# Folded weights ahead of the second half of the input, and that half's projections between the shifts of a convolution

## The chip, the cores and the metric

The kernel is written in Bass and runs on one core of a Trainium2 chip. The metric is the device time of one execution in microseconds (us). TensorE multiplies matrices, VectorE (DVE), ScalarE (ACT) and GpSimd (POOL) work element by element, and SyncE (SP) issues the DMAs. Each engine runs its own instruction list in order and waits on semaphores.

## The reference

The input x has 4 images of 16 x 16 pixels and 128 channels. The first of two layers, cut to what matters here:

```python
x_ln = layernorm(x, ln_g, ln_b)                        # over the 128 channels
q = x_flat @ wq + bq
q_img = q.reshape(b, c, h, w)
o = conv_general_dilated(q_img, dw_w, (2, 2), ..., feature_group_count=c)   # 7x7 depthwise, stride 2
o = gelu(o + dw_b)
offsets = conv_general_dilated(o, pw_w, (1, 1), ...)   # 128 -> 2 channels
deformed = refs + tanh(offsets)
interp = grid_sample_bilinear_zeros(x, grid of deformed)
v = k = interp_flat @ wv + bv
qh = heads(q @ mq_w + mq_b); kh = heads(k @ mk_w + mk_b); vh = heads(v @ mv_w + mv_b)
att = softmax(qh kh^T) vh
z = att @ mo_w + mo_b + x
x = gelu(layernorm(z) @ mlp_w + mlp_b) + z
```

The second layer is a group norm, one attention head of width 128 over the 256 pixels of an image, an output projection and a residual.

## The kernel before, in words

All data fits on chip. x lies in eight tiles of 128 pixels by 128 channels (two tiles an image), and the work up to the sampling goes in two halves of two images, four tiles each. Everything is float32 apart from dummy matmuls on zeros (`keep_warm`, on the bfloat16 tile `warm`). A float32 matmul shows as two passes in the trace, each with a weight load, so 4 matmuls are 8 rows there. The order of every engine is written out by hand.

**Loads.** SP issues (lines 246 to 255) image 0, image 1, the constants `early`, a row of biases, then the second half of x in one DMA of 256 KB (semaphore `x_in2`), then the 320 KB of weights `fold` (`fold_in`), then `gb`, `mid`, `x_st` and `late`.

**Norm and first projection.** DVE takes statistics of the four tiles of a half (`st`, `mv`), ACT takes the square root (`sd`), DVE the reciprocal (`rstd`). The normalized tiles `x_hat` of the first half come from DVE (line 540), those of the second half from ACT (line 363), which needs `shift` from DVE (line 545). TensorE projects each tile with `wq_conv`: one 128 x 128 matmul, in which the tile is the stationary operand (loop at line 872). `qbias_mm` is a bias made by TensorE and copied by ACT to `q_bias`. DVE's `project_images(g)` (line 511) writes `q_conv` for the two images of half g.

**Convolution as matmuls.** `move_half(g)` (line 825) spreads `q_conv` over partitions with 16 matmuls that have 32 output partitions each; ACT and DVE copy the result to `q_ph` (`phases_out`, two phases each). `conv_half(g, first, last)` (line 843) runs shifts first to last-1 of 16 shifts, four matmuls of 32 output partitions a shift, all into bank 5. Their weights `wd` are made by POOL in four chunks (line 280). Moves and shifts show as form `128*32`, full matmuls as `128*128`. After the sixteenth shift of half 0, ACT applies the GELU (`o_act`, line 372), TensorE makes the coordinates (`coord_half`), ACT the tanh, and DVE, ACT the bilinear weights with which TensorE samples x.

**Folded weights.** `fold_keys` (line 860) multiplies `wv` into `mk_w` and `mv_w` (one matmul of 256 columns); `fold_query` (line 865) multiplies `wq` into `mq_w` and makes three bias columns with one-column matmuls. ACT copies `m_kv`, `m_q` and `cols` out of the banks (lines 389 to 398).

**TensorE's order before.** Project tiles 0 to 3 (bias before tile 3), two dummy matmuls, `move_half(0)`, `fold_query`, project tiles 4 to 7, shifts 0 to 5 of half 0, `move_half(1)`, shifts 6 to 15, `fold_keys`, `coord_half(0)`, then the first five shifts of half 1, the queries of half 0, and the sampling. Later stages (scores, softmax, MLP, group norm, second attention) are not touched.

Of the kernel before, what the change touches and what calls it, by code (L numbers as in the profile page):

```python
# [8 lines left out]
ACT = mybir.ActivationFunctionType  # L9
# [3 lines left out]
B, H, W, C = 4, 16, 16, 128  # L13
# [55 lines left out]
def build(nc, x, early, fold, mid, late, rows, ln_rows, out):  # L69
    ctx = ExitStack()  # L70
    with ctx:
# [27 lines left out]
        def r(name):  # L99
# [78 lines left out]
            "loads and constants": """x_in0 x_in1 x_in2 early_in fold_in mid_in late_in rows_in lnrow_in xst_in  # L178
                warm_set ones_set consts vones_set v1ones_set""",
            "norm of x": "stats aggr sdev rstd_ok shift_ok hat_ok hat_a xg_ok xln_ok",  # L180
            "folded weights": """colsum_mm colsum_ok qbias_mm qbias_ok foldq_mm m_q_ok cols_ok foldkv_mm m_kv_ok
                fold1_mm w_vo_ok cols1_ok outbias_mm outbias_ok msabias_mm msabias_ok mlpw_ok gamma_ok""",
            "convolution": """q_mm q_out wd_ok move_a move_v qph_a qph_v conv_mm gelu_ok""",
            "sampling": "coord_mm tanh_ok dx_ok dy_ok fx_ok ay_ok hx_ok hy_ok bilin_ok interp_mm sampled_ok",
# [15 lines left out]
        def halves(h):  # L200
            return slice(4 * h, 4 * h + 4)
# [41 lines left out]
        @block.sync  # L243
        def _(sp):

            for b in range(G):
                sp.dma_start(x_hw[:, S * b:S * b + S, :], x_hw_dram[:, b]).then_inc(s[f"x_in{b}"], 16)  # L247
            sp.dma_start(packs["early"][:, :], early).then_inc(s["early_in"], 16)
            sp.dma_start(row[:, :], rows).then_inc(s["rows_in"], 16)
            sp.dma_start(x_hw[:, halves(1), :].rearrange("p (b s) c -> p b s c", s=S), x_hw_dram[:, G:B]).then_inc(s["x_in2"], 16)  # L250
            sp.dma_start(packs["fold"][:, :], fold).then_inc(s["fold_in"], 16)
            sp.dma_start(gb[:, :], ln_rows.partition_broadcast(P)).then_inc(s["lnrow_in"], 16)
            sp.dma_start(packs["mid"][:, :], mid).then_inc(s["mid_in"], 16)
            sp.dma_start(x_st[:, :, :], x_st_dram).then_inc(s["xst_in"], 16)
            sp.dma_start(packs["late"][:, :], late).then_inc(s["late_in"], 16)

            for b in range(B - 1):
                sp.wait_ge(s["y_ok"], 2 * b + 2)
                sp.dma_start(out_dram[:, b, :], y[:, 2 * b:2 * b + 2, :].rearrange("p s c -> p (s c)")).then_inc(s["y_out"], 16)
            for i in (T - 2, T - 1):  # L260
                sp.wait_ge(s["y_ok"], i + 1)
                t = i % S
                sp.dma_start(out_dram[:, B - 1, t * C:(t + 1) * C], y[:, i, :]).then_inc(s["y_out"], 16)

            sp.wait_ge(s["y_out"], 16 * (B + 1))

        @block.gpsimd
        def _(pool):
# [15 lines left out]
            def norm_affine(h):  # L284
# [63 lines left out]
        def _(act):  # L348
# [6 lines left out]
            act.wait_ge(s["qbias_mm"], 1)  # L355
            act.copy(q_bias[:, :].rearrange("c (r s n) -> c r s n", r=2, s=S),
                     bank[5][:, 0:C].rearrange("c (r n) -> c r n", r=2).unsqueeze(2).to_broadcast([P, 2, S, C // 2])).then_inc(s["qbias_ok"], 1)
            act.wait_ge(s["aggr"], 8)
            act.activation(sd[:, halves(1)], mv[:, halves(1), 1], ACT.Sqrt, bias=eps[:, 0:1]).then_inc(s["sdev"], 1)
            act.wait_ge(s["shift_ok"], 1)  # L360

            for i in range(4, T):
                act.activation(x_hat[:, i], x_hw[:, i], ACT.Identity, scale=rstd[:, i:i + 1],
                               bias=shift[:, i - 4:i - 3]).then_inc(s["hat_a"], 1)

            def phases_out(g):
                act.wait_ge(s["move_a"], g + 1)
# [15 lines left out]
                act.activation(hat_y[:, g].rearrange("p s q -> p (s q)"), abs_y[:, g], ACT.Relu, scale=-1.0, bias=1.0).then_inc(s["hy_ok"], 1)  # L383

            phases_out(0)
            act.activation(scratch[:, 1:2], eps[:, :], ACT.Gelu)
            phases_out(1)
            gelu_half(0)
            act.wait_ge(s["foldkv_mm"], 1)
            act.copy(m_kv[:, :], bank[7][:, 0:2 * C]).then_inc(s["m_kv_ok"], 1)  # L390
            tanh_half(0)

            act.wait_ge(s["foldq_mm"], 1)
            act.copy(m_q[:, :], bank[6][:, 0:C]).then_inc(s["m_q_ok"], 1)
# [115 lines left out]
        def _(dve):  # L510
# [9 lines left out]
                        op0=ALU.mult, op1=ALU.add).then_inc(s["q_out"], 1)  # L520


            for h in range(2):
                for i in range(4 * h, 4 * h + 4):
                    if i in (0, 2, 4):

                        dve.wait_ge(s[f"x_in{i // 2}"], 16)
                    dve.bn_stats(st[:, i], x_hw[:, i]).then_inc(s["stats"], 1)  # L528
                for i in range(4 * h, 4 * h + 4):
                    dve.wait_ge(s["stats"], i + 1)  # L530
                    dve.bn_aggr(mv[:, i], st[:, i]).then_inc(s["aggr"], 1)
                if h == 1:
                    dve.wait_ge(s["early_in"], 16)
                    project_images(0)
                dve.wait_ge(s["sdev"], h + 1)
                dve.reciprocal(rstd[:, halves(h)], sd[:, halves(h)]).then_inc(s["rstd_ok"], 1)
                dve.wait_ge(s["rstd_ok"], h + 1)
                if h == 0:
                    for i in range(4):
                        dve.tensor_scalar(x_hat[:, i], x_hw[:, i], mv[:, i, 0:1], rstd[:, i:i + 1], ALU.subtract, ALU.mult).then_inc(s["hat_ok"], 1)  # L540
                    dve.wait_ge(s["colsum_mm"], 1)
                    dve.tensor_copy(colsum[:, :], bank[5][0:1, 0:C]).then_inc(s["colsum_ok"], 1)
                else:

                    dve.scalar_tensor_tensor(out=shift[:, :], in0=mv[:, halves(1), 0], scalar=-1.0, in1=rstd[:, halves(1)],
                                             op0=ALU.mult, op1=ALU.mult).then_inc(s["shift_ok"], 1)

            def phases_out(g):
                dve.wait_ge(s["move_v"], g + 1)
                dve.tensor_copy(q_ph[:, g, 2:4].rearrange("p k n -> p (k n)"), bank[4][:, 0:2 * G * PIX]).then_inc(s["qph_v"], 1)  # L550

            phases_out(0)
            project_images(1)
            phases_out(1)

# [252 lines left out]
        def _(pe):  # L808
# [13 lines left out]
            mm(bank[5][0:1, 0:C], ones_col[:, :], w("wq_conv")).then_inc(s["colsum_mm"], 1)  # L822
            keep_warm(2)

            def move_half(g):

                pe.wait_ge(s["q_out"], G * g + G)
                if g == 1:

                    pe.wait_ge(s["qph_a"], 1)  # L830
                    pe.wait_ge(s["qph_v"], 1)
                src = q_conv[:, g].rearrange("c (r yb t x) -> c r yb t x", r=2, t=2, x=OW)
                for k in range(PHASES):
                    at = (k % 2) * G * PIX
                    for f in range(PHASES):
                        m = mm(bank[3 + k // 2][f * BLK:(f + 1) * BLK, at:at + G * PIX].rearrange("p (yb x) -> p yb x", x=OW),
                               w("ident")[:, k * BLK:(k + 1) * BLK], src[:, f // 2, :, f % 2])
                    if k == 1:
                        m.then_inc(s["move_a"], 1)
                    if k == 3:  # L840
                        m.then_inc(s["move_v"], 1)
# [22 lines left out]

            def fold_query():
                pe.wait_ge(s["fold_in"], 16)
                mm(bank[6][:, 0:C], w("wqT"), w("mq_w"))
                mm(bank[6][:, C:C + 1], w("mq_w"), w("bq"))
                mm(bank[6][:, C + 1:C + 2], w("mk_w"), w("bv"))
                mm(bank[6][:, C + 2:C + 3], w("mv_w"), w("bv")).then_inc(s["foldq_mm"], 1)  # L870

            for i in range(T):
                b, t = divmod(i, S)
                if i == 3:

                    pe.wait_ge(s["colsum_ok"], 1)
                    pe.wait_ge(s["rows_in"], 16)
                    mm(bank[5][:, 0:C], r("ln_b"), colsum[:, :], stop=False)
                    mm(bank[5][:, 0:C], ones_row[:, :], r("bq_conv"), start=False).then_inc(s["qbias_mm"], 1)
                if i == 4:  # L880
                    keep_warm(2)
                    move_half(0)
                    fold_query()

                if i < 4:
                    pe.wait_ge(s["hat_ok"], i + 1)
                else:
                    pe.wait_ge(s["hat_a"], i - 3)
                o = query_image(b).rearrange("c (r s n) -> c r s n", r=2, s=S)[:, :, t]
                m = mm(o, x_hat[:, i], w("wq_conv"))  # L890
                if t == S - 1:
                    m.then_inc(s["q_mm"], 1)

            def query_half(h):
                pe.wait_ge(s["m_q_ok"], 1)
# [133 lines left out]
                mm(bank[3 + b][:, 0:HW], mlp_wg[:, :], z_t[:, 2 * b:2 * b + 2, :].rearrange("c s q -> c (s q)")).then_inc(s["mlp_mm"], 1)  # L1029

            N = len(SHIFTS)
            conv_half(0, 0, 6)
            move_half(1)
            conv_half(0, 6, N)
            fold_keys()
            coord_half(0)
            conv_half(1, 0, 5)
            query_half(0)
# [254 lines left out]
```

## Time and profile before

| | us |
|---|---|
| runs | 79.25, 79.36, 79.98; median 79.36 |
| the profiled execution | 79.27 |
| its span, first to last instruction | 77.4 |
| around the span | 1.87 |
| PE, DVE, ACT, POOL busy | 70.6, 51.7, 33.9, 24.3 |

The span is what the instructions of the program cover. Of the 77.4 us, this case concerns the stretch from about 2.5 to 19 us. A pass of TensorE has a modelled end: its next pass starts before that end when the two overlap in the array.

### The profile page before, as it was taken

Reading aid. Unit: us, or ns where it says so; the run is one execution under the profiler, and the core shown is the slowest. Engines: PE = TensorE matmul, PEld = TensorE weight load, DVE = VectorE, ACT = ScalarE, POOL = GpSimd, SP = SyncE. Lnnn points to the kernel's source line nnn. Section 1 sums busy time; section 2 is a strip of 40 time slices with the busy share of each in tenths; the row PEclk is TensorE's granted clock in tenths of the full one; section 3 lists DMA queues with packets and bytes.
Section 4 is the critical chain, followed back from the end, with each engine's and each line's share of the span. In section 5 each row is a group of like instructions: output and inputs, shape, how many; then the busy total and the mean of one; then the engine's idle time right before and its main releaser. Section 6 shows DMA issues by size and latency. Waiting matters only on the chain.

```text
span 77.4 us, 1968 instructions
## 1 busy us (share of the span) xinstructions
PE 70.6 (91%) x732; PEld 53.6 (69%) x732; DVE 51.7 (67%) x172; ACT 33.9 (44%) x84; POOL 24.3 (31%) x37
## 2 busy tenths in 40 slices
PE   4999699998999999999999999998897999998950
PEld 2345599783786647879777989845485869996830
DVE  0478742116366959477789968599799786868480
ACT  6112397068139563524424419820248048263600
POOL 5008999900000038390019137123820030000000
PEclk9999999999999999999999999999999999999999
DMA  0789870000000000000000000000000000010112
GB/s 9 226 270 150 305 289 12 0 8 0 0 8 0 0 0 4 0 0 8 0 0 0 4 0 0 8 0 0 0 0 0 0 0 4 0 68 9 59 55 89
DMA packets 3051, 3.07 MB, mean 40 GB/s; under 512 B 225, under 2 KB 2657, under 8 KB 3042
## 3 DMA queue, kind: packets, MB, share of 16 engines
q1 hardware_dynamic: 3042, 2.95, 12.8%
q8 instruction: 6, 0.10, 0.5%
q14 instruction: 3, 0.02, 0.1%
HBM read 2.42 MB, written 0.52 MB: 38 GB/s over the span
## 4 chain that ended last, share of the span: by engine, by line
PE 63%; DVE 17%; issue 5%; DMA 5%; ACT 3%; SPq 2%; POOL 2%; DVEq 0%; POOLq 0%; ACTq 0%
PE bank L810 53%; DMA x_hw<-x 5%; PE bank L971 5%; PE bank L1140 2%; DVE smax L604 2%; DVE x_t L656 1%; DVE gst L694 1%; SPq L247 1%; DVE st L528 1%; DVE bilin L578 1%; DVE x_gn L716 1%; DVE dist_y L562 1%; PE bank L989 1%; DVE q_conv L517 1%; POOL grs L330 1%
## 5 line engine op out<-in xcount | busy, mean ns | idle before, releaser
L810 PE MATMUL bank<-k_blk,qh 128*128 128x512 f32 x16 | 8.4, 605 | 0.0
L810 PE MATMUL bank<-v_blk,p_t 128*128 128x34 f32 x64 | 7.8, 267 | 0.0
L810 PEld LDWEIGHTS bank<-v_blk,p_t 128*128 128x128 f32 x64 | 7.8, 192 | 0.0
L810 PE MATMUL bank<-warm 128*128 128x512 bf16 x18 | 6.3, 471 | 1.0 <-POOL warm L269 1.0
L604 DVE TENSOR_REDUCE smax<-bank 128x8 f32<-128x512 f32 x8 | 5.5, 685 | 2.4 <-PE bank L810 2.4
L317 POOL TENSOR_TENSOR zrs<-zve,neg_half 128x2 f32<-128x2 f32 x4 | 2.9, 714 | 12.7 <-DVE zve L646 12.7
L810 PE MATMUL bank<-q_ph,wd 128*32 128x112 f32 (+5 forms) x256 | 6.8, 249 | 0.0
L303 POOL TENSOR_TENSOR x_res<-x_st,msa_bias 128x1024 f32<-128x1024 f32 x1 | 2.4, 2358 | 12.8 <-DVE bilin L578 12.8
L431 ACT ACTIVATE p_t<-bank 128x512 f32<-128x512 f32 x8 | 4.8, 597 | 3.4 <-PE bank L971 3.4
L810 PEld LDWEIGHTS bank<-q_ph,wd 128*32 128x32 f32 x256 | 5.6, 109 | 0.7 <-issue 0.3
L611 DVE TENSOR_TENSOR s_sub<-bank,smax 128x512 f32<-128x512 f32 x8 | 5.5, 682 | 0.1
L280 POOL TENSOR_TENSOR wd<-pack_early 128x512 f32<-128x512 f32 x4 | 4.1, 1046 | 4.4 <-DVE x_hat L540 4.4
L810 PE MATMUL bank<-v,p_t 128*128 128x129 f32 x32 | 4.8, 284 | 0.6 <-ACT p_t L233 0.4
L810 PEld LDWEIGHTS bank<-v,p_t 128*128 128x128 f32 x32 | 4.2, 190 | 1.2 <-issue 1.0
L971 PE MATMUL bank<-pack_early,s_sub 128*128 128x128 f32 x32 | 5.0, 279 | 0.0
L488 ACT ACTIVATE p<-bank,nmax 128x256 f32<-128x256 f32 x8 | 3.4, 476 | 3.0 <-DVE nmax L728 2.8
L438 ACT COPY att_t<-bank 128x128 f32<-128x128 f32 x8 | 2.1, 263 | 5.4 <-PE bank L989 5.3
L971 PEld LDWEIGHTS bank<-pack_early,s_sub 128*128 128x128 f32 x32 | 3.7, 144 | 0.8 <-issue 0.5
L810 PE MATMUL bank<-k,q 128*128 128x256 f32 x16 | 4.2, 385 | 0.0
L528 DVE BATCH_NORM_STATS2 st<-x_hw 128x6 f32<-128x128 f32 x8 | 1.8, 283 | 3.2 <-DMA x_hw<-x 3.2
L810 PEld LDWEIGHTS bank<-warm 128*128 128x128 bf16 x18 | 2.0, 122 | 2.9 <-issue 1.9
L810 PE MATMUL bank<-pack_mid,att_t 128*128 128x128 f32 x16 | 3.7, 311 | 0.2 <-DVE z L634 0.2
(149 smaller groups left out, 161.2 us busy)
## 6 DMA issues: line engine op xcount, KB each, us to landing
x_st<-x SPq DMA_DIRECT2D x1, 512.0 KB, 6.7
pack_late<-late SPq DMA_DIRECT2D x1, 448.0 KB, 7.3
out<-y SPq DMA_DIRECT2D x3, 128.0 KB, 1.7
pack_fold<-fold SPq DMA_DIRECT2D x1, 320.0 KB, 4.1
pack_mid<-mid SPq DMA_DIRECT2D x1, 261.0 KB, 5.8
x_hw<-x SPq DMA_DIRECT2D x2, 128.0 KB, 2.2
x_hw<-x SPq DMA_DIRECT2D x1, 256.0 KB, 3.8
pack_early<-early SPq DMA_DIRECT2D x1, 184.0 KB, 2.5
```

The costliest lines, as they stand in the source:

```text
L280: pool.tensor_tensor(wd[:, n:n + WD_CHUNK].rearrange("p n k j -> p (n k) j"), w("ident32").unsqueeze(1).to_broadcast([P, WD_CHUNK * PHASES ...
L303: pool.tensor_tensor(x_res[:, :, :], x_st[:, :, :].rearrange("p b (s c) -> p (b s) c", s=S), msa_bias[:, :].unsqueeze(1).to_broadcast([P, ...
L317: pool.tensor_tensor(zrs[:, 2 * b:2 * b + 2], zve[:, 2 * b:2 * b + 2], neg_half[:, 0:2], ALU.pow).then_inc(s["zrs_ok"], 1)
L431: act.activation(p_t[:, i % 2].rearrange("p j q -> p (j q)"), bank[5 + i % 2][:, :], ACT.Exp).then_inc(s["exp_ok"], 1)
L438: act.copy(att_t[:, i % 2], bank[0][:, 0:P]).then_inc(s["attt_ok"], 1)
L488: act.activation(p1[:, b % 2, t], bank[5 + b % 2][:, t * HW:(t + 1) * HW], ACT.Exp, bias=nmax1[:, 2 * b + t:2 * b + t + 1]).then_inc(s["p1 ...
L528: dve.bn_stats(st[:, i], x_hw[:, i]).then_inc(s["stats"], 1)
L604: dve.tensor_reduce(smax[:, i % 2], scores(i), AX.X, ALU.max).then_inc(s["smax_ok"], 1)
L611: dve.tensor_tensor(s_sub[:, i % 2], scores(i), smax[:, i % 2].unsqueeze(2).to_broadcast([P, NH, PIX]), ALU.subtract).then_inc(s["ssub_ok" ...
L810: return pe.matmul(o, l, r_, start=start, stop=stop, **k)
L971: m = pe.transpose(bank[5 + i % 2][:, j * P:(j + 1) * P], s_sub[:, i % 2, 2 * j:2 * j + 2].rearrange("p h q -> p (h q)"), w("ident"))
L1140: m = pe.transpose(bank[(2, 0)[t]][:, j * P:(j + 1) * P], p1[:, b % 2, t, j * P:(j + 1) * P], w("ident"))
```

## The change

SP issues `fold` ahead of the second half of x. On TensorE the two dummy matmuls ahead of the first move go; both folds stand in their place, and the three bias columns follow the first move as `fold_columns`, with a wait for `m_q_ok` since they share a bank with the product that ACT copies. The projections of tiles 4 to 7 go between shifts of half 0 (after 5, 7, 9 and 11 shifts), and `move_half(1)` is cut in two: phases 0 and 1 after 14 shifts, phases 2 and 3 after the sixteenth. On DVE `project_images(0)` goes ahead of the second half's statistics, and the scale and shift of the second half go behind `phases_out(0)`. ACT copies `m_kv` and `m_q` ahead of `phases_out(0)` and makes the four `x_hat` tiles behind it. POOL waits for `shift_ok` before its `norm_affine(0)`. The amount of arithmetic is the same apart from the two dummy matmuls.

```diff
             sp.dma_start(row[:, :], rows).then_inc(s["rows_in"], 16)
+            sp.dma_start(packs["fold"][:, :], fold).then_inc(s["fold_in"], 16)
             sp.dma_start(x_hw[:, halves(1), :].rearrange("p (b s) c -> p b s c", s=S), x_hw_dram[:, G:B]).then_inc(s["x_in2"], 16)
-            sp.dma_start(packs["fold"][:, :], fold).then_inc(s["fold_in"], 16)
...
+            pool.wait_ge(s["shift_ok"], 1)
             norm_affine(0)
...
-            act.wait_ge(s["aggr"], 8)
...
+            act.wait_ge(s["foldkv_mm"], 1)
+            act.copy(m_kv[:, :], bank[7][:, 0:2 * C]).then_inc(s["m_kv_ok"], 1)
+            act.wait_ge(s["foldq_mm"], 1)
+            act.copy(m_q[:, :], bank[6][:, 0:C]).then_inc(s["m_q_ok"], 1)
...
             phases_out(0)
+            act.wait_ge(s["aggr"], 8)
...
+            dve.wait_ge(s["early_in"], 16)
+            project_images(0)
+            input_stats(1)
             phases_out(0)
+            input_scale(1)
...
+            for i in range(3):
+                project_tile(i)
...
+            project_tile(3)
+            fold_keys()
+            fold_query()
+            move_half(0)
+            fold_columns()
...
-            conv_half(0, 0, 6)
-            move_half(1)
-            conv_half(0, 6, N)
-            fold_keys()
+            conv_half(0, 0, 5)
+            project_tile(4)
+            conv_half(0, 5, 7)
+            project_tile(5)
+            conv_half(0, 7, 9)
+            project_tile(6)
+            conv_half(0, 9, 11)
+            project_tile(7)
+            conv_half(0, 11, 14)
+            move_half(1, range(0, 2))
+            conv_half(0, 14, N)
+            move_half(1, range(2, 4))
             coord_half(0)
```

TensorE before, from the last tile of the first half to the coordinates (`pack_fold` are the folds, `q_conv` the moves, `q_ph,wd` the shifts, `o_act` the coordinates):

```order
8 L810 MATMUL bank<-pack_early,x_hat 128x2x64 [waits hat_ok]
9 L810 MATMUL bank<-warm 128x512 x2
10 L810 MATMUL bank<-q_conv,pack_early 32x128 [waits q_out]
11 L810 MATMUL bank<-q_conv,pack_early 32x128 x15
12 L810 MATMUL bank<-pack_fold 128x128 [waits fold_in]
13 L810 MATMUL bank<-pack_early,pack_fold 128x1 x3
14 L810 MATMUL bank<-pack_early,x_hat 128x2x64 [waits hat_a] x4
15 L810 MATMUL bank<-q_ph,wd 32x128 [waits wd_ok,qph_v,qph_a]
...
36 L810 MATMUL bank<-pack_fold 128x256 [waits fold_in]
37 L810 MATMUL bank<-o_act,pack_early 128x128 [waits gelu_ok]
```

And the same engine in the changed kernel, up to the third of the four projections that now stand among the shifts:

```order
8 L814 MATMUL bank<-pack_early,x_hat 128x2x64 [waits hat_ok]
9 L814 MATMUL bank<-pack_fold 128x256 [waits fold_in]
10 L814 MATMUL bank<-pack_fold 128x128 [waits fold_in]
11 L814 MATMUL bank<-q_conv,pack_early 32x128 [waits q_out]
12 L814 MATMUL bank<-q_conv,pack_early 32x128 x15
13 L814 MATMUL bank<-pack_early,pack_fold 128x1 [waits m_q_ok]
...
22 L814 MATMUL bank<-pack_early,x_hat 128x2x64 [waits hat_a]
23 L814 MATMUL bank<-q_ph,wd 32x14x6 x4
24 L814 MATMUL bank<-q_ph,wd 32x14x7 x4
25 L814 MATMUL bank<-pack_early,x_hat 128x2x64 [waits hat_a]
26 L814 MATMUL bank<-q_ph,wd 32x112 x4
27 L814 MATMUL bank<-q_ph,wd 32x14x7 [waits wd_ok]
```

The two folds took the place of the dummy matmuls, and each projection of the second half now stands alone between matmuls with 32 output partitions.

DVE before, in the same stretch (`st` and `mv` are the second half's statistics, `q_ph` the copy that the first shift needs):

```order
10 L528 BN_STATS st<-x_hw 128x6 [waits x_in2]
11 L528 BN_STATS st<-x_hw 128x6 x3
12 L531 BN_AGGR mv<-st 128x2 [waits stats] x4
13 L517 SCALAR_TENSOR_TENSOR q_conv<-bank,pack_early,q_bias 128x16x16 [waits q_mm,qbias_ok,early_in]
14 L517 SCALAR_TENSOR_TENSOR q_conv<-bank,pack_early,q_bias 128x16x16 [waits q_mm]
15 L536 RECIPROCAL rstd<-sd 128x4 [waits sdev]
16 L545 SCALAR_TENSOR_TENSOR shift<-mv,rstd 128x4 [waits rstd_ok]
17 L550 COPY q_ph<-bank 128x256 [waits move_v]
```

DVE in the changed kernel:

```order
10 L518 SCALAR_TENSOR_TENSOR q_conv<-bank,pack_early,q_bias 128x16x16 [waits q_mm,qbias_ok,early_in]
11 L518 SCALAR_TENSOR_TENSOR q_conv<-bank,pack_early,q_bias 128x16x16 [waits q_mm]
12 L529 BN_STATS st<-x_hw 128x6 [waits x_in2]
13 L529 BN_STATS st<-x_hw 128x6 x3
14 L532 BN_AGGR mv<-st 128x2 [waits stats] x4
15 L541 COPY q_ph<-bank 128x256 [waits move_v]
16 L536 RECIPROCAL rstd<-sd 128x4 [waits sdev]
17 L555 SCALAR_TENSOR_TENSOR shift<-mv,rstd 128x4 [waits rstd_ok]
```

The statistics moved behind the first half's `q_conv`, and the reciprocal and `shift` behind the copy to `q_ph`.

## Rows read from the trace of the kernel before

**Rows 1.** The page: busy time, and the granted clock in forty slices.

```profile
PE 70.6 (91%) x732; PEld 53.6 (69%) x732; DVE 51.7 (67%) x172; ACT 33.9 (44%) x84; POOL 24.3 (31%) x37
PEclk9999999999999999999999999999999999999999
```

**Rows 2.** Chain that ended last, in time: start us, us, what.

```profile
2.58 3.76 DMA x_hw<-x
...
8.38 6.58 PE bank L810 x195
```

**Rows 3.** Timeline of TensorE: start us, us, what, count [idle before].

```profile
6.80 0.49 PE L810 MATMUL bank<-pack_early,x_hat 128*128 128x128 f32 x2
7.13 0.59 PE L810 MATMUL bank<-warm 128*128 128x512 bf16 x2
8.38 1.08 PE L810 MATMUL bank<-q_conv,pack_early 128*32 128x128 f32 x32 [0.65 <-DVE q_conv L517]
9.39 0.49 PE L810 MATMUL bank<-pack_fold 128*128 128x128 f32 x2
9.71 0.73 PE L810 MATMUL bank<-pack_early,pack_fold 128*128 128x1 f32 x6
10.30 1.14 PE L810 MATMUL bank<-pack_early,x_hat 128*128 128x128 f32 x8
11.37 1.15 PE L810 MATMUL bank<-q_ph,wd 128*32 128x128 f32 x48
12.34 1.06 PE L810 MATMUL bank<-q_conv,pack_early 128*32 128x128 f32 x32
13.21 2.35 PE L810 MATMUL bank<-q_ph,wd 128*32 128x98 f32 x80
15.49 0.70 PE L810 MATMUL bank<-pack_fold 128*128 128x256 f32 x2
16.02 0.71 PE L810 MATMUL bank<-o_act,pack_early 128*128 128x128 f32 x4
19.72 0.71 PE L810 MATMUL bank<-q_ph,wd 128*32 128x84 f32 x24
20.36 0.49 PE L810 MATMUL bank<-sampled,m_kv 128*128 128x128 f32 x2
20.78 0.45 PE L810 MATMUL bank<-m_kv,sampled 128*64 128x64 f32 x8
```

**Rows 4.** Timeline of ScalarE, same columns.

```profile
6.91 0.37 ACT L356 COPY q_bias<-bank 128x256 f32<-128x256 f32 x1 [2.35 <-PE bank L810]
9.18 1.65 ACT L363 ACTIVATE x_hat<-x_hw,shift,rstd 128x128 f32<-128x128 f32 x4 [1.33 <-DVE shift L545]
15.61 0.37 ACT L372 ACTIVATE o_act<-bank,pack_early 128x128 f32<-128x128 f32 x1 [2.21 <-PE bank L810]
```

**Rows 5.** Timeline of VectorE, same columns.

```profile
6.36 0.87 DVE L528 BATCH_NORM_STATS2 st<-x_hw 128x6 f32<-128x128 f32 x4 [0.25 <-DMA x_hw<-x]
7.16 0.36 DVE L531 BATCH_NORM_AGGREGATE mv<-st 128x2 f32<-128x6 f32 x4
7.45 0.88 DVE L517 SCALAR_TENSOR_TENSOR q_conv<-bank,pack_early,q_bias 128x256 f32<-128x256 f32 x2
8.44 0.71 DVE L545 SCALAR_TENSOR_TENSOR shift<-mv,rstd 128x4 f32<-128x4 f32 x1
9.53 0.42 DVE L550 COPY q_ph<-bank 128x256 f32<-128x256 f32 x1 [0.38 <-PE bank L810]
```

**Rows 6.** Timeline of GpSimd: the convolution weights, four chunks.

```profile
6.08 4.06 POOL L280 TENSOR_TENSOR wd<-pack_early 128x512 f32<-128x512 f32 x4 [4.42 <-DVE x_hat L540]
```

**Rows 7.** DMA issues, KB and us from issue to landing; before them SyncE's issue of fold.

```profile
3.01 0.50 SPq L251 DMA_DIRECT2D pack_fold<-fold  x1
...
pack_fold<-fold SPq DMA_DIRECT2D x1, 320.0 KB, 4.1
gb<-ln_rows SPq DMA_DIRECT2D x1, 128.0 KB, 5.0
```

More of the change, by code:

```diff
@@ L180, in build @@
             "norm of x": "stats aggr sdev rstd_ok shift_ok hat_ok hat_a xg_ok xln_ok",
-            "folded weights": """colsum_mm colsum_ok qbias_mm qbias_ok foldq_mm m_q_ok cols_ok foldkv_mm m_kv_ok
+            "folded weights": """colsum_mm colsum_ok qbias_mm qbias_ok foldq_mm foldc_mm m_q_ok cols_ok foldkv_mm m_kv_ok
                 fold1_mm w_vo_ok cols1_ok outbias_mm outbias_ok msabias_mm msabias_ok mlpw_ok gamma_ok""",
@@ L357, in _ @@
                      bank[5][:, 0:C].rearrange("c (r n) -> c r n", r=2).unsqueeze(2).to_broadcast([P, 2, S, C // 2])).then_inc(s["qbias_ok"], 1)
-            act.wait_ge(s["aggr"], 8)
[L359 to L364, printed above, removed]
+            act.wait_ge(s["foldkv_mm"], 1)
+            act.copy(m_kv[:, :], bank[7][:, 0:2 * C]).then_inc(s["m_kv_ok"], 1)
+            act.wait_ge(s["foldq_mm"], 1)
+            act.copy(m_q[:, :], bank[6][:, 0:C]).then_inc(s["m_q_ok"], 1)
             def phases_out(g):
@@ L385, in _ @@
             phases_out(0)
+            act.wait_ge(s["aggr"], 8)
+            act.activation(sd[:, halves(1)], mv[:, halves(1), 1], ACT.Sqrt, bias=eps[:, 0:1]).then_inc(s["sdev"], 1)
+            act.wait_ge(s["shift_ok"], 1)
+            for i in range(4, T):
+                act.activation(x_hat[:, i], x_hw[:, i], ACT.Identity, scale=rstd[:, i:i + 1],
+                               bias=shift[:, i - 4:i - 3]).then_inc(s["hat_a"], 1)
             act.activation(scratch[:, 1:2], eps[:, :], ACT.Gelu)
@@ L388, in _ @@
             gelu_half(0)
-            act.wait_ge(s["foldkv_mm"], 1)
-            act.copy(m_kv[:, :], bank[7][:, 0:2 * C]).then_inc(s["m_kv_ok"], 1)
             tanh_half(0)
-            act.wait_ge(s["foldq_mm"], 1)
-            act.copy(m_q[:, :], bank[6][:, 0:C]).then_inc(s["m_q_ok"], 1)
             hats_half(0)
+            act.wait_ge(s["foldc_mm"], 1)
             for j, name in enumerate(("mq_b", "mk_b", "mv_b")):
@@ L520, in project_images, with input_stats @@
                         op0=ALU.mult, op1=ALU.add).then_inc(s["q_out"], 1)
-            for h in range(2):
+            def input_stats(h):
                 for i in range(4 * h, 4 * h + 4):
@@ L531, in _, with input_scale @@
                     dve.bn_aggr(mv[:, i], st[:, i]).then_inc(s["aggr"], 1)
-                if h == 1:
-                    dve.wait_ge(s["early_in"], 16)
-                    project_images(0)
+            def input_scale(h):
                 dve.wait_ge(s["sdev"], h + 1)
@@ L537, in _ @@
                 dve.wait_ge(s["rstd_ok"], h + 1)
[L538 to L546, printed above, removed]
             def phases_out(g):
@@ L550, in phases_out @@
                 dve.tensor_copy(q_ph[:, g, 2:4].rearrange("p k n -> p (k n)"), bank[4][:, 0:2 * G * PIX]).then_inc(s["qph_v"], 1)
+            input_stats(0)
+            input_scale(0)
+            for i in range(4):
+                dve.tensor_scalar(x_hat[:, i], x_hw[:, i], mv[:, i, 0:1], rstd[:, i:i + 1], ALU.subtract, ALU.mult).then_inc(s["hat_ok"], 1)
+            dve.wait_ge(s["colsum_mm"], 1)
+            dve.tensor_copy(colsum[:, :], bank[5][0:1, 0:C]).then_inc(s["colsum_ok"], 1)
+            dve.wait_ge(s["early_in"], 16)
+            project_images(0)
+            input_stats(1)
             phases_out(0)
+            input_scale(1)
+            dve.scalar_tensor_tensor(out=shift[:, :], in0=mv[:, halves(1), 0], scalar=-1.0, in1=rstd[:, halves(1)],
+                                     op0=ALU.mult, op1=ALU.mult).then_inc(s["shift_ok"], 1)
             project_images(1)
@@ L823, in _, with move_half @@
             keep_warm(2)
-            def move_half(g):
+            def move_half(g, phases=range(PHASES)):
                 pe.wait_ge(s["q_out"], G * g + G)
@@ L832, in move_half @@
                 src = q_conv[:, g].rearrange("c (r yb t x) -> c r yb t x", r=2, t=2, x=OW)
-                for k in range(PHASES):
+                for k in phases:
                     at = (k % 2) * G * PIX
@@ L866, in fold_query, with fold_columns, project_tile @@
                 pe.wait_ge(s["fold_in"], 16)
-                mm(bank[6][:, 0:C], w("wqT"), w("mq_w"))
+                mm(bank[6][:, 0:C], w("wqT"), w("mq_w")).then_inc(s["foldq_mm"], 1)
+            def fold_columns():
+                pe.wait_ge(s["m_q_ok"], 1)
                 mm(bank[6][:, C:C + 1], w("mq_w"), w("bq"))
                 mm(bank[6][:, C + 1:C + 2], w("mk_w"), w("bv"))
-                mm(bank[6][:, C + 2:C + 3], w("mv_w"), w("bv")).then_inc(s["foldq_mm"], 1)
-            for i in range(T):
+                mm(bank[6][:, C + 2:C + 3], w("mv_w"), w("bv")).then_inc(s["foldc_mm"], 1)
+            def project_tile(i):
                 b, t = divmod(i, S)
[L874 to L883, printed above, removed]
                 if i < 4:
@@ L892, in _ @@
                     m.then_inc(s["q_mm"], 1)
+            for i in range(3):
+                project_tile(i)
+            pe.wait_ge(s["colsum_ok"], 1)
+            pe.wait_ge(s["rows_in"], 16)
+            mm(bank[5][:, 0:C], r("ln_b"), colsum[:, :], stop=False)
+            mm(bank[5][:, 0:C], ones_row[:, :], r("bq_conv"), start=False).then_inc(s["qbias_mm"], 1)
+            project_tile(3)
[3 more added lines that the diff above has]
+            fold_columns()
             def query_half(h):
```

## The prediction

> **What bounds the kernel now.** I read the busy time by engine first: TensorE is busy for 70.6 of 77.4 us, with VectorE next at 51.7, and the granted clock is at its upper level (2.4 GHz) in all forty slices [rows 1]. Then the chain that ended last: it comes from the landing of x's second half at 6.34 us (2.58 + 3.76), through VectorE's statistics and `q_conv`, to TensorE at 8.38, and stays on TensorE for 195 passes [rows 2]. Then TensorE's timeline, which tells which of its work stands in front of the convolution's end [rows 3]. From 8.38 to 16.02 it idles nowhere for a wait: move 8.38, fold 9.39, columns 9.71, four projected tiles 10.30, six shifts 11.37, the second move 12.34, ten shifts 13.21 (ending 13.21 + 2.35 = 15.56). What follows hangs on that end: the GELU runs 15.61 to 15.98 [rows 4] and the coordinates start at 16.02. `fold_keys`, at 15.49, stands in the GELU's shadow and costs nothing where it is. So the question is when the sixteenth shift of half 0 ends. All later stages wait for things derived from it, with nothing else late there, so they move by the same amount; I found nothing of theirs that the change touches.
>
> **The head of the stretch.** `q_bias` is ready at 6.91 + 0.37 = 7.28 [rows 4], but `q_conv` starts only at 7.45, since VectorE is on the statistics [rows 5]. Changed, it starts at 7.32 and ends at 7.32 + 0.88 = 8.20; TensorE's first move follows at 8.25 instead of 8.38. The gain is 0.13. The folds must fit ahead of it. They start at 7.13, where the dummy matmuls do, if `fold` has landed: issued at 2.58 instead of 3.01, with 4.1 to landing [rows 7], it lands by 6.7 (2.58 + 3.76 = 6.3 by the other transfer of about that size [rows 2]). Added without overlap, 0.70 and 0.49 [rows 3] end at 8.32, but a pass of the same form starts about 0.16 before the modelled end of the last, so 8.0 is nearer; the next form may start then. They cost nothing. If they were late by 0.1 the move is late by 0.1. Without the dummies TensorE idles 0.25 here; the idle 0.65 of before [rows 3] did not lower the granted clock [rows 1], so I charge nothing.
>
> **From the first move to the first shift.** Move: 8.25 + 1.08 = 9.33. The columns start 0.07 before that (the move's row ends at 9.46, the next starts at 9.39 [rows 3]), at 9.26; `m_q`, which they wait for, is copied about 8.25 to 8.55. They keep TensorE 0.73, plus 0.09 because the first pass after a change of form waits for its weights (see below): 10.08 to 10.17. The shifts start 0.07 before that, 10.10. Is VectorE in time? Statistics run 6.36 to 7.52 in before, 1.16 [rows 5]; behind `q_conv` they end at 8.20 + 1.18 = 9.38. The last move pass ends about 9.33 and the copy to `q_ph` takes 0.42 [rows 5], so it is done at 9.82. It binds nothing, with 0.28 to spare. POOL's first chunk of weights is long there [rows 6]. First shift: 10.10 instead of 11.37, a gain of 1.27, of which the four tiles that went elsewhere are 1.07 (10.30 to 11.37).
>
> **What a projected tile costs among the shifts.** This decides the case. Within one form the next row starts well before the modelled end of the one before: shifts end 11.37 + 1.15 = 12.52, the move starts 12.34, 0.18 earlier. Where the form changes, the overlap is 0.07 each time: shifts end 20.43 and the full matmul starts 20.36; it ends 20.85 and the next form starts 20.78; the tiles end 11.44 and the shifts start 11.37 [rows 3]. A lone 128 x 128 matmul is 0.49 (20.36), while in a row of four it is 1.07 / 4 = 0.27. So let shifts end at E. The tile starts at E - 0.07, ends at E + 0.42, and the next shift starts at E + 0.35. Without the tile it would have started at E - 0.18. That is 0.53, and I take 0.55 because the first weights of the new form are not loaded ahead. Four tiles: 2.20, against 1.07 where they stood. Its bounds: 0.27 (the in-row slot) and 0.67 (no overlap at all: 0.49 + 0.18).
>
> What the rows show is thus a price of some 0.11 for each change between 32, 64 and 128 output partitions, and the change adds eight of them. The Trainium skill, "TensorEngine Tiling (Array Packing)", Key Properties, says the same in principle: changing the tiling mode, not just the tile, drains TensorE. By that rule no clever order of independent work hides it and 0.55 stands; without the rule, a tile at 0.27 is open and the sum below would be 1.1 lower. The trace agrees with the rule at every change of form that I looked at.
>
> **The second move.** Before, all of it (12.34 to 13.21, 0.87) stands ahead of the last shift. Now half does; the other half runs in the GELU's shadow. The GELU path from the last shift's end to the coordinates is 16.02 - 15.56 = 0.46, and half a move is 0.44. Gain 0.43, and the coordinates stay bound by the GELU. VectorE's copy of that half (0.42) ends about 0.9 after the last shift, and the first shift of half 1 comes 1.1 after it (16.02 + 0.71 - 0.07 = 16.66, less 15.56), so it is covered too, by 0.2.
>
> **The waits that are added.** Tile 4 needs ACT's first `x_hat`. VectorE makes `shift` after the copy: reciprocal 9.84 to 10.01, shift from 10.04. Before, `shift` took 0.71 for 4 columns, from 8.44 to 9.15, while POOL worked at `wd` [rows 5, 6]; POOL's third chunk (four in 4.06) ends at about 9.13. The fourth ends at 10.14, and now POOL then waits, so I let `shift` end by 10.25, and the first `x_hat` by 10.75 (four take 1.65 [rows 4], about 0.48 for one). TensorE gets to tile 4 at 10.10 + 5 x 0.16 = 10.90 (six shifts took 11.37 to 12.34). No wait, 0.15 to spare. The other tiles come every 0.4 for ACT and every 0.9 for TensorE. Behind ACT's tiles stands one table load, as before, and its next copy is not due before about 15. POOL's part of the queries comes 0.1 to 0.2 later and is needed only after five shifts of half 1.
> `shift` reads two SBUF tiles. The Trainium skill, "SBUF — State Buffer", Who interferes with whom, has VectorE's instructions with two SBUF inputs held off by a GpSimd instruction until it is over. The row agrees with that (0.71, ending with a chunk); by it `shift` is done just after 10.14, otherwise it would be 0.71 by itself and end at 10.75, which is rival 3.
> The move at 14 shifts needs `q_conv` of image 3: after tile 7 VectorE takes about 0.48 for one image plus 0.07 of signalling; TensorE has three shifts, about 0.5, less the 0.07 overlap. I charge 0.10.
>
> **The sum.** End of shift sixteen: 10.10 + 4.19 (11.37 to 15.56) - 0.43 + 2.20 + 0.10 = 16.16, against 15.56: 0.60 later. The parts: head and tiles moved away -1.27, half move -0.43, four lone tiles +2.20, wait +0.10. The profiled execution took 79.27 (span 77.4, 1.87 around it), so 79.87, said as 79.9. The runs' median, 79.36, is 0.09 above the profiled one; against it the forecast is +0.7%, inside the 1% (0.79 us) that a measurement of this kernel can tell from no change.
>
> **Rivals.**
> 1. *The change of form is hidden*: shifts and tile are independent and a tile costs its in-row 0.27. Then 4 x 0.27 = 1.08 in place of 2.20: 16.16 - 1.12 = 15.04, 0.52 earlier, 78.75; by start-to-start times a tile in a row is less (a pair of passes is 0.49 and eight are 1.14, so six more are 0.65, or 0.22 a tile), which takes 0.20 more, to 78.55. For it: rows only show modelled ends. Against: starts are measured, and 20.36 to 20.78 is this very pattern.
> 2. *x's second half lands late* and VectorE's in-order queue then holds back the copy to `q_ph`, which before did not stand behind that data. Issued at about 3.1, with 3.76 it lands at 6.9; with the 5.0 of the transfer behind it [rows 7] at 8.1. It decides from 10.10 - 0.04 - 0.42 - 0.04 - 1.16 = 8.44 on, one for one. At 9.8 the end would be 1.36 later: 81.2. Against: 320 KB ahead of it instead of behind is a bandwidth matter of 1 us at most, as fold landed 0.8 after it before.
> 3. *`shift` is slow by itself*, 0.71 wherever it stands: first `x_hat` at 10.75 + 0.03 + 0.48 = 11.26, TensorE waits 0.35 at tile 4, the sum is 80.2. This is slower than before by 1.1%. It decides from a first `x_hat` after 10.90. For it: I have the one row.
> 4. *The fold lands too late* for 7.13: every tenth past 7.4 delays the first move by one. At before's 7.1 it costs nothing, so 79.9 stays.
>
> **How the numbers follow.** The forecast has 0.62, within 79.5 to 80.4: the tile price may be 0.50 or 0.60 (0.2 each way) and small waits add up to 0.2. About a fifth of it lies above 80.15. Rival 1 has 0.15, most of it faster by over 1%. Rival 3 has 0.13, two thirds of it slower by over 1%. Rival 2 has 0.05, all slower. Rival 4 and what I don't see have 0.05, nearly all within 1%. Faster: 0.12 + 0.01 = 0.13. Slower: 0.13 + 0.09 + 0.05 = 0.27. Same: 0.60. The range, 79.0 to 80.6, takes in the tile at about 0.35 below and rival 3 with small waits above; it leaves out rival 1 in full and rival 2.
>
> **What would show it.** In the changed profile: moves start at 8.25; the first shift at 10.1 (11.37 before); each `x_hat` pair of passes between shifts spans 0.49 with 0.07 of overlap on both sides; the last shift of half 0 ends near 16.2 and the coordinates start near 16.6; the sampling is 0.6 later, and so is every later stage. The forecast is wrong if a lone tile takes less than 0.4 from shift to shift, if the first shift starts after 10.3, or if some later stage doesn't move with the sampling.

## The result and the profile after

The changed kernel takes 79.95 us in the median (79.51 to 80.36, 20 runs), the kernel before 79.42 (78.95 to 80.00, 20 runs): ratio 1.0061, 95% interval 1.0037 to 1.0085. It is slower by 0.6%, a half microsecond. The profiled execution took 80.20, its span is 78.4. The medians and ratios of this document leave out executions that took over 1.5% more than the fastest of the same kernel.

TensorE after, in the stretch of [rows 3] (columns as there):

```profile
7.62 0.49 PE L814 MATMUL bank<-pack_early,x_hat 128*128 128x128 f32 x2
7.95 0.82 PE L814 MATMUL bank<-pack_fold 128*128 128x256 f32 x4
9.18 1.08 PE L814 MATMUL bank<-q_conv,pack_early 128*32 128x128 f32 x32 [0.42 <-DVE q_conv L518]
10.19 0.83 PE L814 MATMUL bank<-pack_early,pack_fold 128*128 128x1 f32 x6
10.95 1.01 PE L814 MATMUL bank<-q_ph,wd 128*32 128x128 f32 x40
11.89 0.49 PE L814 MATMUL bank<-pack_early,x_hat 128*128 128x128 f32 x2
12.31 0.52 PE L814 MATMUL bank<-q_ph,wd 128*32 128x84 f32 x16
...
14.59 0.49 PE L814 MATMUL bank<-pack_early,x_hat 128*128 128x128 f32 x2
15.01 0.71 PE L814 MATMUL bank<-q_ph,wd 128*32 128x112 f32 x24
15.65 0.65 PE L814 MATMUL bank<-q_conv,pack_early 128*32 128x128 f32 x16
16.11 0.55 PE L814 MATMUL bank<-q_ph,wd 128*32 128x112 f32 x16
16.47 0.62 PE L814 MATMUL bank<-q_conv,pack_early 128*32 128x128 f32 x16
17.14 0.71 PE L814 MATMUL bank<-o_act,pack_early 128*128 128x128 f32 x4
...
20.21 0.70 PE L814 MATMUL bank<-x_hw,bilin 128*64 128x64 f32 x16 [0.37 <-DVE bilin L582]
```

VectorE after, answering to [rows 5]:

```profile
8.25 0.88 DVE L518 SCALAR_TENSOR_TENSOR q_conv<-bank,pack_early,q_bias 128x256 f32<-128x256 f32 x2 [2.21 <-PE bank L814]
9.05 0.86 DVE L529 BATCH_NORM_STATS2 st<-x_hw 128x6 f32<-128x128 f32 x4
...
10.33 0.42 DVE L541 COPY q_ph<-bank 128x256 f32<-128x256 f32 x1
10.67 0.17 DVE L536 RECIPROCAL rstd<-sd 128x4 f32<-128x4 f32 x1
10.88 0.16 DVE L555 SCALAR_TENSOR_TENSOR shift<-mv,rstd 128x4 f32<-128x4 f32 x1
...
15.11 0.48 DVE L518 SCALAR_TENSOR_TENSOR q_conv<-bank,pack_early,q_bias 128x256 f32<-128x256 f32 x1 [1.26 <-PE bank L814]
```

ScalarE after, answering to [rows 4], and the landing of the fold:

```profile
11.07 1.65 ACT L389 ACTIVATE x_hat<-x_hw,shift,rstd 128x128 f32<-128x128 f32 x4 [0.55 <-DVE shift L555]
...
16.36 0.37 ACT L366 COPY q_ph<-bank 128x256 f32<-128x256 f32 x1 [2.13 <-PE bank L814]
16.73 0.37 ACT L370 ACTIVATE o_act<-bank,pack_early 128x128 f32<-128x128 f32 x1
```

```profile
pack_fold<-fold SPq DMA_DIRECT2D x1, 320.0 KB, 3.7
```

Absolute times mislead here. The first move starts at 9.18 against 8.38 [rows 3], yet the tile three places ahead of it starts at 7.62 against 6.80: 0.8 us were already lost in front of the first instruction that differs on TensorE. The two dummy matmuls before the first tiles show where. This is the kernel before, and after:

```profile
4.68 0.60 PE L810 MATMUL bank<-warm 128*128 128x512 bf16 x2
```

```profile
5.02 1.03 PE L814 MATMUL bank<-warm 128*128 128x512 bf16 x2
```

The same two instructions take 0.60 in one profile and 1.03 in the other. It is not work that the change added, since TensorE's instructions up to there are the same in both kernels (more on it at the end). So I read every profile from the start of the first move, and call the time from there to the coordinates "the stretch". It is 16.02 - 8.38 = 7.64 in the first profile of before and 17.14 - 9.18 = 7.96 after. From the coordinates to the sampling both have 3.07, and from the sampling to the end of the span 58.3 and 58.2: nothing later answers to the change.

In the stretch, the first shift starts 1.77 after the first move (2.99 before). From the first shift to the end of the sixteenth it takes 16.66 - 10.95 = 5.71 (4.19 before). A tile among the shifts reads 11.89 to 12.38, with 0.07 of overlap with its neighbour on each side.

### The profile page after: what moved, and what is told of

It is laid out like the page before. It is cut to its first block, busy times and chain, and to the rows that moved or that the text cites. A ratio compares the mean times of both kernels' runs of the same rounds, so it can differ in the third digit from the quotient of the medians.

```text
span 78.4 us, 1965 instructions
## 1 busy us (share of the span) xinstructions
PE 72.1 (92%) x730; PEld 54.1 (69%) x730; DVE 51.3 (65%) x172; ACT 33.9 (43%) x84; POOL 24.3 (31%) x37
## 2 busy tenths in 40 slices
DMA packets 3051, 3.07 MB, mean 39 GB/s; under 512 B 225, under 2 KB 2657, under 8 KB 3042
## 4 chain that ended last, share of the span: by engine, by line
PE 70%; DVE 15%; issue 5%; ACT 4%; POOL 2%; DVEq 0%; POOLq 0%; ACTq 0%
PE bank L814 61%; PE bank L979 5%; PE bank L1156 2%; DVE smax L608 2%; DVE x_t L660 1%; DVE gst L698 1%; DVE q_conv L518 1%; DVE bilin L582 1%; DVE x_gn L720 1%; DVE dist_y L566 1%; PE bank L997 1%; POOL grs L331 1%; DVE s_sub L615 1%; POOL zrs L318 1%; DVE x_res L665 1%
## 5 line engine op out<-in xcount | busy, mean ns | idle before, releaser
L814 PE MATMUL bank<-q_ph,wd 128*32 128x84 f32 (+5 forms) x256 | 7.2, 251 | 0.0
L518 DVE SCALAR_TENSOR_TENSOR q_conv<-bank,pack_early,q_bias 128x256 f32<-128x256 f32 x4 | 1.8, 481 | 5.8 <-PE bank L814 5.8
```

The source lines that it names most:

```text
L518: dve.scalar_tensor_tensor(out=q_conv[:, g].rearrange("c (n b x) -> c n b x", b=G, x=R * OW)[:, :, b % G], in0=query_image(b).rearrange("c ...
L814: return pe.matmul(o, l, r_, start=start, stop=stop, **k)
```

## The experiments

Ratios are to the kernel before, timed on the same chip. The stretch is from each one's profile. e9, a single timed run of e5's kernel, stands with e5 below.

| kernel | median us | ratio, interval | stretch us |
|---|---|---|---|
| changed | 79.95 | 1.0061 (1.0037 to 1.0085) | 7.96 |
| e1 one block | 78.83 | 0.9930 (0.9898 to 0.9963) | 6.82 |
| e11 two pairs | 79.26 | 0.9969 (0.9937 to 1.0001) | 7.30 |
| e2 move whole | 80.28 | 1.0123 (1.0085 to 1.0160) | 8.39 |
| e3 four extra, spread | 81.56 | 1.0282 (1.0233 to 1.0331) | 9.48 |
| e4 four extra, together | 80.20 | 1.0102 (1.0061 to 1.0143) | 8.48 |
| e10 before again | one run, 78.94 | | 7.25 |
| e6 before, fold first | 79.53 | 1.0022 (0.9994 to 1.0050) | 7.25 |
| e7 changed, x first | 80.20 | 1.0107 (1.0064 to 1.0151) | 7.96 |
| e5 no POOL wait | 80.45 | 1.0162 (1.0114 to 1.0210) | 7.96 |
| e8 block, keys late | 78.85 | 0.9931 (0.9902 to 0.9961) | 6.73 |

**e1: the four tiles in one block.**

```diff
-            conv_half(0, 0, 5)
-            project_tile(4)
...
-            conv_half(0, 9, 11)
-            project_tile(7)
-            conv_half(0, 11, 14)
+            conv_half(0, 0, 9)
+            for i in range(4, T):
+                project_tile(i)
+            conv_half(0, 9, 14)
```

> The changed kernel with the four projections of the second half in one block after nine shifts, in place of four places. My theory (each change of form costs about 0.11 us, so three tiles fall from 0.55 to 0.22 us): 1.0 us less than the changed kernel, 78.9 to 79.0, ratio to before about 0.994. A small loss of 0.1 is possible if the moves wait for q_conv of image 3. If instead the loss came from something else (the DMA order, the split move, the removed dummy matmuls), it stays at 79.9 to 80.0, ratio 1.006.

Measured 78.83, 1.1 us less than the changed kernel. The shifts, the block and the shifts behind it, of this kernel:

```profile
10.58 1.68 PE L814 MATMUL bank<-q_ph,wd 128*32 128x128 f32 x72
12.19 1.16 PE L814 MATMUL bank<-pack_early,x_hat 128*128 128x128 f32 x8
13.28 1.07 PE L814 MATMUL bank<-q_ph,wd 128*32 128x96 f32 x40
```

Four tiles take 1.09 from start to the next start; spread out each takes 0.42 plus a lost overlap. This kernel beats both, and before by 0.7%.

**e11: two pairs** (tiles 4 and 5 after 7 shifts, 6 and 7 after 11).

```diff
-            conv_half(0, 0, 5)
-            project_tile(4)
...
+            conv_half(0, 0, 7)
+            project_tile(4)
+            project_tile(5)
+            conv_half(0, 7, 11)
+            project_tile(6)
+            project_tile(7)
```

> The changed kernel with the four projections in two pairs, after 7 and after 11 shifts: two pairs of form changes fewer than the changed kernel, one pair more than the block. Theory (0.33 us for each pair of changes): first move to coordinates 7.96 - 0.66 = 7.30 in the profile (the wait for image 3 may add 0.15 or less), 79.3 in the median, ratio 0.999. Rival (only the number of places beyond one matters, or the wait for q_conv carried the gain of the block): 78.9 or 79.9.

The stretch is 16.27 - 8.97 = 7.30, as expected, and the median 79.26. Four places, two places, one place: 7.96, 7.30, 6.82. The first two places given up are worth 0.33 each, the third 0.48. Of that the wait for image 3 is 0.15: it is in the two spread kernels and not in the block, where the move starts 0.19 before the shifts ahead of it end.

```profile
11.99 0.71 PE L814 MATMUL bank<-pack_early,x_hat 128*128 128x128 f32 x4
12.63 0.92 PE L814 MATMUL bank<-q_ph,wd 128*32 128x112 f32 x32
...
16.27 0.71 PE L814 MATMUL bank<-o_act,pack_early 128*128 128x128 f32 x4
```

**e3 and e4: the price by itself.** Four matmuls whose result nobody reads, in the kernel before.

```diff
+            def extra():
+                mm(bank[7][:, 2 * C:3 * C], w("ident"), w("wq_conv"))
...
-            conv_half(0, 6, N)
+            conv_half(0, 6, 7)
+            extra()
+            conv_half(0, 7, 9)
+            extra()
...
```

> The kernel before with four extra full matmuls of 128 x 128 (result unused, bank 7), each alone between shifts of half 0 (after 7, 9, 11 and 13). Measures the disputed price by itself. My theory: 4 x 0.55 = 2.2 us more, 81.6, ratio 1.028. Rival (a change of form is hidden): 4 x 0.22 = 0.9 us, 80.3, ratio 1.011.

> The kernel before with the same four extra matmuls in one block after nine shifts. My theory: 0.55 + 3 x 0.22 = 1.2 us more, 80.6, ratio 1.015, so 1.0 us less than spread. Rival (a change of form is hidden): the same 80.3 as spread.

Against the stretch of 7.25 of the kernel before (e10), spread costs 9.48 - 7.25 = 2.23 and together 8.48 - 7.25 = 1.23. The medians, against 79.28 for the kernel before on that chip, say 2.3 and 0.9. The 0.9 is under the 1.2 that was expected and that the profile shows, and its interval (0.5 to 1.1) leaves 1.2 out; why the timed runs lost less stays open. The rival is out all the same: equal work in another order differs by 1.0 in the stretches and by 1.4 in the medians. One extra of the spread kernel, then the block of the other:

```profile
13.77 0.49 PE L810 MATMUL bank<-pack_early 128*128 128x128 f32 x2
14.19 0.57 PE L810 MATMUL bank<-q_ph,wd 128*32 128x112 f32 x16
```

```profile
14.33 1.16 PE L810 MATMUL bank<-pack_early 128*128 128x128 f32 x8
15.42 1.43 PE L810 MATMUL bank<-q_ph,wd 128*32 128x96 f32 x56
```

**e2: the second move whole.**

```diff
-            move_half(1, range(0, 2))
-            conv_half(0, 14, N)
-            move_half(1, range(2, 4))
+            move_half(1)
+            conv_half(0, 14, N)
```

> The changed kernel with the second move whole, after 14 shifts, so that no half of it runs in the GELU's shadow. My theory: the second half of the move stands ahead of the last shift again, 0.43 us more than the changed kernel, 80.4, ratio 1.012. Rival (the coordinates are held by ScalarE's copy of q_ph ahead of the GELU, or the whole is bound elsewhere): no more than 0.1 us of difference.

Measured 80.28. That is 1.00 above the kernel before on its chip, where the changed kernel is 0.53 above, so 0.47 more, and 8.39 - 7.96 = 0.43 in the stretch. The half in the GELU's shadow is really hidden: without it TensorE idles 0.49 there.

```profile
16.15 0.54 PE L814 MATMUL bank<-q_ph,wd 128*32 128x112 f32 x16
17.18 0.71 PE L814 MATMUL bank<-o_act,pack_early 128*128 128x128 f32 x4 [0.49 <-ACT o_act L370]
```

**e10: before again.** No edit.

> The kernel before, unchanged, for a second profile. In the first one shifts 6 to 15 of half 0 took 2.28 us from start to the fold behind them, with a gap of 0.28 that nothing released; the same stretch took 1.86 with the fold's DMA moved. If the gap is a chance of that one run, first move to coordinates takes 7.25 here instead of 7.64, and the changed kernel's 7.96 is 0.71 longer. If it belongs to the kernel, 7.64 again.

The gap did not come again. The first row starts 1.86 before the fold behind it, where [rows 3] has 2.28:

```profile
13.26 1.93 PE L810 MATMUL bank<-q_ph,wd 128*32 128x98 f32 x80
15.12 0.70 PE L810 MATMUL bank<-pack_fold 128*128 128x256 f32 x2
```

In the first profile of before, the gap shows among the weight loads (PEld) of the same shifts:

```profile
13.10 1.62 PEld L810 LDWEIGHTS bank<-q_ph,wd 128*32 128x32 f32 x68
15.00 0.34 PEld L810 LDWEIGHTS bank<-q_ph,wd 128*32 128x32 f32 x12 [0.28 <-issue]
```

So the changed kernel's stretch is 7.96 - 7.25 = 0.71 longer, not 0.32.

**e6 and e7: the order of the DMAs alone**, in before and in the changed kernel (the second swaps them back).

```diff
+            sp.dma_start(packs["fold"][:, :], fold).then_inc(s["fold_in"], 16)
             sp.dma_start(x_hw[:, halves(1), :].rearrange("p (b s) c -> p b s c", s=S), x_hw_dram[:, G:B]).then_inc(s["x_in2"], 16)
-            sp.dma_start(packs["fold"][:, :], fold).then_inc(s["fold_in"], 16)
```

> The kernel before with the fold's DMA ahead of the second half of x, and nothing else. VectorE still takes the statistics first. Theory: the second half lands at about 6.95 instead of 6.34, statistics end at 8.1 instead of 7.5, q_conv starts at 8.1 instead of 7.45 where the clock rose early, so 0.2 to 0.6 us more, 79.7, ratio 1.005. Rival (the order of the DMAs costs nothing because TensorE's bias is as late): 79.3, ratio 1.000.

> The changed kernel with x's second half ahead of the fold again. Theory: the fold lands at about 7.1, when TensorE gets to it at 7.1 to 7.9, so nothing moves: 79.9, ratio 1.006. Rival (the DMA order carries part of the loss or hides part of a gain): 0.3 us or more either way.

Neither can be told from its parent: 1.0022 (0.9994 to 1.0050) against 1, and 1.0107 against 1.0061 with overlapping intervals and the same stretch. In e6 VectorE's statistics start at 7.06, when the second half of x lands, and `q_conv` starts at 8.13, about 0.1 after it could. In e7 the fold landed at about 7.7 (4.7 after its issue), later than the 7.1 expected, and cost nothing since TensorE reached it at 8.02. The order of the DMAs is not where the half microsecond is.

**e5 and e9: without GpSimd's wait.**

```diff
-            pool.wait_ge(s["shift_ok"], 1)
```

> The changed kernel without GpSimd's wait for shift_ok ahead of norm_affine(0). Theory (VectorE's instruction with two SBUF inputs is held off by GpSimd's): x_g starts at about 10.1, shift is held until it ends at about 11.4 and takes up to 1 us by the profile instead of 0.16, the first x_hat of ScalarE ends at about 11.9, and TensorE waits 0 to 0.8 us at tile 4, by where its head stands: 80.3, ratio 1.011. Rival (no such hold, shift's 0.71 in before was its own): shift 0.16 as in the changed kernel, 79.95, ratio 1.006.

> The kernel of the fifth experiment once more, for a profile in which x arrives at its usual time. Theory: GpSimd's x_g starts at about 10.1, ahead of shift, and shift is shown with 0.3 to 1.0 us instead of 0.16, ending as x_g ends; ScalarE's x_hat tiles and TensorE's tile 4 follow late. Rival: shift shows 0.16 while x_g is running.

The four timed runs of e5 have a median of 80.45 and an interval that lies above the changed kernel's, though not above that of e7 (1.0064 to 1.0151), which was timed on the same chip. Neither profile shows the hold, and both have the changed kernel's stretch of 7.96. In both, `shift` started just ahead of `x_g` and took 0.16 while `x_g` ran. By the letter that is the rival of both expectations; it doesn't show what happens when `x_g` comes first. VectorE and GpSimd of e9:

```profile
10.35 0.16 DVE L554 SCALAR_TENSOR_TENSOR shift<-mv,rstd 128x4 f32<-128x4 f32 x1
```

```profile
10.38 1.29 POOL L290 TENSOR_TENSOR x_g<-x_hat,gb 128x512 f32<-128x512 f32 x1
```

That the slower runs are those in which `x_g` came first is my guess, and stays open. Its one further run took 79.78.

**e8: the columns ahead of the first move, the keys behind the coordinates**, on top of e1. The query product goes to bank 7, and the copies and waits follow it; the cut shows TensorE's order.

```diff
-            fold_keys()
             fold_query()
+            fold_columns()
             move_half(0)
-            fold_columns()
...
             coord_half(0)
+            fold_keys()
```

> The block kernel (first experiment of this study) with the bias columns ahead of the first move, the query product in bank 7, and fold_keys behind the coordinates, where TensorE waits 0.37 us for the bilinear weights anyway. Theory: the first move starts where it did, the first shift is held by VectorE's copy alone and starts 1.6 us after the first move instead of 1.77, the keys cost 0.06: 0.1 us less than the block kernel, 78.7, ratio 0.992. Rival (the keys behind the coordinates hold back the tanh path or the sampling): 0.1 to 0.4 us more than the block kernel.

The stretch is 0.09 shorter, as expected (the first shift starts 1.68 after the first move for the 1.6 foretold), and the keys cost nothing behind the coordinates (3.07 to the sampling, as in e1). The medians, 78.85 and 78.83, cannot show a tenth. I count it as no gain.

## Why the prediction was right, and where it wasn't

The forecast was 79.9, +0.60 on the profiled run; measured are 79.95 and a difference of 0.53 between the medians (0.3 to 0.7 by the interval). In the profiles, from tile 3 to the coordinates, it is 0.69: 0.71 in the stretch less 0.02 ahead of it. What the timed runs have less than the profiles stays open, and that 0.60 lies so near is in part luck, since the forecast has the head 0.13 and a wait 0.05 too cheap, and the columns 0.08 too dear. By the steps of the forecast:

**The price of a tile among the shifts: right.** It was 0.55 each, read from one lone matmul of another stage. The same 0.42 from start to next start and the same 0.07 overlaps stand in the changed profile. e3 measured 2.23 for four (2.20 foretold), e4 1.23 for the block; e1 and e11 took the price back in steps. A pair of changes thus costs 0.33. What a change of form looks like shows among the weight loads. At a change the load starts with the pass that needs it; here is tile 4 of the changed kernel, whose first pass starts at 11.89:

```profile
11.89 0.30 PEld L814 LDWEIGHTS bank<-pack_early,x_hat 128*128 128x128 f32 x2
```

Between two groups of one form it starts ahead: the load at 13.10 shown under e10 belongs to shifts that start at 13.21 [rows 3], 0.11 later. Another bank and other operands alone are not what costs: that same place goes from moves to shifts and keeps its overlap of 0.19 (12.34 + 1.06 - 13.21). The rule of the Trainium skill that I had weighed ("TensorEngine Tiling (Array Packing)", Key Properties: a change of tiling mode drains TensorE) agrees with these rows. They show a later start, not the draining itself.

**The second move: right.** 0.43 foretold, 0.43 by e2.

**The waits: right.** At tile 4 there is none: `x_hat` is ready at about 11.07 + 0.48 = 11.55 and TensorE comes at 11.89, 0.34 to spare for the 0.15 foretold. `shift` takes 0.16 with GpSimd idle, where it took 0.71 beside `wd` [rows 5, 6] and 0.72 in e10:

```profile
8.49 0.72 DVE L545 SCALAR_TENSOR_TENSOR shift<-mv,rstd 128x4 f32<-128x4 f32 x1
```

So rival 3 is out. In before, e10 and e6 `shift` ends at 9.15, 9.21 and 9.74, each time 0.02 after GpSimd's third chunk of `wd`, whatever its start. These rows agree with the Trainium skill, "SBUF — State Buffer", Who interferes with whom: a VectorE instruction with two SBUF inputs contends with a GpSimd instruction that reads SBUF. Whether GpSimd's wait for `shift_ok` is needed stays open with e5. The wait for image 3 was 0.15 for 0.10: `q_conv` ends at 15.11 + 0.48 = 15.59 and the move starts at 15.65. The fold landed at 2.58 + 3.7 = 6.3 and held nothing. Rival 2 is out as well: x's second half landed at about 7.0, and at about 8.0 in e11, each time before VectorE had finished `q_conv` and could use it (9.05 and 8.83).

**The head: wrong by 0.13.** I had taken `q_conv`'s start at 7.45 as held by the statistics. But tile 3 ends at 6.80 + 0.49 = 7.29 [rows 3], and `q_conv` waits for that too: after, 7.62 + 0.49 = 8.11 and `q_conv` at 8.25, the same 0.15 later. VectorE had two reasons for 7.45, and taking one away gave nothing. e10 shows it without the change: there the statistics were over at 7.23, and `q_conv` still waited for TensorE, whose tile 3 ends at 6.87 + 0.49 = 7.36:

```profile
7.50 0.88 DVE L517 SCALAR_TENSOR_TENSOR q_conv<-bank,pack_early,q_bias 128x256 f32<-128x256 f32 x2 [0.27 <-PE bank L810]
```

From tile 3 to the first move it is 1.58 before and 1.56 after.

**The columns: 0.08 too dear.** The first shift starts 1.77 after the first move for 1.85 foretold. The recorded time of the columns' end is 10.08 to 10.17, and the sum went on from 10.17: that charges the 0.09 for the change of form twice. From 10.08, less the overlap of 0.07, it is 10.01 - 8.25 = 1.76.

**A gap of one run, carried twice.** My 4.19 from the first shift to the last end holds 0.42 that the kernel doesn't have in e10. It went into both sides of the difference and cancelled. The stretch was foretold as 16.16 + 0.46 - 8.25 = 8.37 and is 7.96, the difference being that gap; the difference between the kernels was foretold as 0.73 in the stretch and is 0.71.

**Where the gain went.** From the first move to the first shift 2.99 - 1.77 = 1.22 went, but 1.07 of it is the four tiles that went elsewhere; the query fold that went into the idle time saves 0.32, and the columns, now between other forms, take 0.17 of that back. Half a move vanishes behind the GELU, 0.43. Against these 1.65, the four tiles come back at about 0.55 each, 2.2, with a wait of 0.15. Put in one block (e1), they leave a gain of 0.7% over the kernel before.

## What to carry to other kernels

Before work is spread as filler between tiled matmuls, read what one lone matmul of the other form costs from start to next start, not what it costs in a row of its like: here 0.55 against 0.22 us. Keep matmuls of one form together. By the same price, work that is put into a wait of TensorE is free only where the wait also covers the two changes of form; no run here tested that. Read differences from an anchor inside the trace, and take a second profile of the kernel before ahead of trusting a gap that nothing released.

## What the runs showed that I had not expected

The profiles differ by up to 0.9 us ahead of the first move, in instructions that are alike: tile 3 starts between 6.80 (before) and 7.70 (e7). Part is when the inputs land, part is TensorE's pace. The first dummy matmuls of 512 columns start 0.43 apart, which is 1.2 columns a ns and fits 1.2 GHz, and later ones 0.22, which fits 2.4, while the granted clock stands at full throughout [rows 1]. The pace rises at about 3.9 us in the kernel before's first profile and between 6 and 7 in the changed one's. TensorE had been at work since 0.98 in both:

```profile
0.98 3.28 PE L810 MATMUL bank<-warm 128*128 128x512 bf16 x8 [0.98 <-POOL warm L269]
```

```profile
0.98 3.59 PE L814 MATMUL bank<-warm 128*128 128x512 bf16 x8 [0.98 <-POOL warm L269]
```

What it is worth shows in e9, which differs from the changed kernel by GpSimd's wait alone. In both profiles the instruction behind these eight starts at 4.50. In e9 the pace rises at about 5.0 and tile 3 starts 0.53 earlier than the changed kernel's 7.62:

```profile
5.02 0.61 PE L813 MATMUL bank<-warm 128*128 128x512 bf16 x2
...
7.09 0.49 PE L813 MATMUL bank<-pack_early,x_hat 128*128 128x128 f32 x2
```

The spans are 77.9 and 78.4, so this makes a run half a microsecond longer or shorter, as much as the whole effect of the change. What decides the moment stays open, and I can't call it chance: in the five profiles of the kernel before and of those built on it (e3, e4, e6, e10) the first eight dummy matmuls take 3.27 to 3.54, in all eight of the changed kernel and of those built on it 3.59 or 3.60, so the pace rose later there each time. The medians don't show such a handicap, since their difference of 0.53 is smaller than that of the stretches. The gap of 0.28 with no releaser in the first profile of before, with which the ten shifts took 0.42 longer, did not come again in e3, e4, e6 or e10; its cause stays open too.
